# A perceiver layer with mixture-of-experts: four expert buffer sets, accumulating stores, new step orders

## The reference, cut to what matters

```python
x = x + xattn(layernorm(x), ctx)   # 16 heads, 64 batches of 32 queries on 257 context rows
x = x + attn(layernorm(x))         # causal, 16 query and 4 key heads of 16, ternary weights
x = x + moe(layernorm(x))
# moe: xt has T = 2048 rows of 256; 8 experts of capacity C = 256; hidden 352 (padded to 384)
probs = softmax(xt @ Wg); eidx = argmax(probs); gate = probs[eidx]
pos = rank of the row among the rows of its expert;  keep = pos < C
flat = where(keep, eidx * C + pos, E * C)
xd = zeros((E * C, d)).at[flat].set(xt, mode='drop')
oe = (silu(xd @ W1) * (xd @ W3)) @ W2                      # per expert
out = oe[min(flat, E * C - 1)] * (gate * keep) + silu(xt @ sw1) * (xt @ sw3) @ sw2
```

## Time and profile before

| | us |
|---|---|
| runs | 1545.86, 1538.57, 1541.29 |
| median | 1541.29 |
| profiled execution | 1538.1 |
| its span | 1536.3 |
| mean granted PE clock | 0.936 |

### The profile page before, as it was taken

How to read it: one execution, slowest core, us unless ns; L and a number is a source line. 1 busy time by engine, 2 the same in 40 slices (tenths; PEclk the granted TensorE clock), 3 DMA queues, 4 the chain that set the end, 5 groups by cost and what they waited for, 6 DMA issues and landing times.

```text
span 1536.3 us, 35628 instructions
## 1 busy us (share of the span) xinstructions
PE 1295.5 (84%) x10526; PEld 881.2 (57%) x10526; DVE 1005.7 (65%) x3748; ACT 841.6 (55%) x3560; POOL 538.5 (35%) x1337
## 2 busy tenths in 40 slices
PE   5768898989899898989898989888898989864881
PEld 2545666566666556565666565656565565643761
DVE  6846677677767677777777776777776767743112
ACT  5365566656475656666565666475656556631110
POOL 2044342524352534435243525342524325310003
PEclk9998999999999999999999999999999989985996
DMA  9000000000010101000001000000101000100544
GB/s 372 22 26 12 23 15 25 17 25 17 11 32 10 32 7 30 13 25 17 21 14 28 14 25 18 14 28 11 31 7 35 7 25 14 62 6 23 168 146 127
DMA packets 41191, 59.65 MB, mean 39 GB/s; under 512 B 5094, under 2 KB 35953, under 8 KB 40096
## 3 DMA queue, kind: packets, MB, share of 16 engines
q1 hardware_dynamic: 36880, 50.73, 10.3%
q0 software_dynamic: 2064, 6.14, 1.2%
q10 hardware_dynamic: 2176, 2.10, 0.4%
HBM read 48.62 MB, written 10.49 MB: 38 GB/s over the span
## 4 chain that ended last, share of the span: by engine, by line
PE 33%; issue 25%; POOL 16%; DVE 9%; ACT 5%; DMA 3%; POOLq 1%; SPq 0%; DVEq 0%; ACTq 0%
PE AB L594 21%; PE Eb L594 5%; POOL prob L1177 4%; PE Db L594 4%; ACT prob L1020 2%; DMA ctxn<-expert_rows 2%; POOL pjunk L1132 2%; PE C L719 1%; POOL cn_lo L1197 1%; DVE o_halves L1492 1%; POOL rstd L1152 1%; ACT rkb L1014 1%; POOL cl_rows L1212 1%; POOL c_lo L1138 1%; DVE kst L1312 1%
## 5 line engine op out<-in xcount | busy, mean ns | idle before, releaser
L950 ACT ACTIVATE AB<-AB 128x128 f32<-128x128 f32 (+1 forms) x1160 | 303.7, 262 | 185.4 <-PE AB L594 182.9
L1132 POOL TENSOR_TENSOR pjunk<-pjunk 128x1 f32<-128x1 f32 x288 | 56.3, 196 | 683.9 <-DVE sinv L1482 365.9
L594 PE MATMUL AB<-wk_hi,c_hi 128*128 128x512 f16 x512 | 199.7, 390 | 22.0 <-POOL c_lo L1138 8.8
L1312 DVE BATCH_NORM_STATS2 kst<-AB 128x6 f32<-128x256 f32 x512 | 181.3, 415 | 55.4 <-PE AB L594 50.9
L950 ACT ACTIVATION_READ_ACCUMULATOR AB<-AB 128x1 f32 (+1 forms) x1160 | 216.0, 186 | 0.0
L594 PE MATMUL AB<-wk_lo,c_hi 128*128 128x512 f16 x512 | 198.5, 388 | 0.0
L594 PE MATMUL AB<-wk_hi,c_lo 128*128 128x512 f16 x512 | 197.5, 386 | 0.0
L594 PE MATMUL AB<-ctxT,qpT 128*128 128x257 f32 x512 | 161.6, 472 | 35.5 <-DVE sc L1547 27.4
L1020 ACT ACTIVATE prob<-prob,nbias,rq 128x257 f32<-128x257 f32 x256 | 150.4, 590 | 7.9 <-DVE nbias L1477 7.9
L594 PEld LDWEIGHTS AB<-ctxT,qpT 128*128 128x128 f32 x512 | 115.2, 236 | 60.6 <-DVE sc L1547 29.1
L1177 POOL TENSOR_SCALAR prob<-prob,sinv 128x257 f32<-128x257 f32 x256 | 128.7, 503 | 20.2
(11 more groups left out here) (252 smaller groups left out, 2933.9 us busy)
## 6 DMA issues: line engine op xcount, KB each, us to landing
ctxT<-in_ctxT SPq DMA_DIRECT2D x64, 128.5 KB, 2.1
ctxn<-in_ctxn SPq DMA_DIRECT2D x64, 128.0 KB, 2.1
wq_hi<-in_w SPq DMA_DIRECT2D x4, 768.0 KB, 5.3
wq_lo<-in_w SPq DMA_DIRECT2D x4, 768.0 KB, 5.6
expert_rows<-base POOLq DMA_DIRECT2D x1, 2048.0 KB, 15.8
xin<-in_x SPq DMA_DIRECT2D x16, 128.0 KB, 2.2
prob<-in_wqT SPq DMA_DIRECT2D x1, 2048.0 KB, 19.2
xres<-in_x SPq DMA_DIRECT2D x16, 128.0 KB, 2.0
```

The source lines that it names most:

```text
L594: return pe.matmul(out, lhsT, rhs, start=start, stop=stop)
L950: ins = nc.scalar.activation(k, k, ACT.Square, accum_out=sums[0:m, h:h + 1])
L1132: own.mark(pool.tensor_tensor(pjunk[:, 0:1], pjunk[:, 1:2], pjunk[:, 1:2], ALU.mult))
L1312: ins = V.bn_stats(stats[:, 0, 2 * half + n], AB[0:m, 2 + half, 2 * D * n:2 * D * (n + 1)])
```

## The change

Three things.

Experts: four sets of buffers (`SETS`), made of weights and tiles that are free by then; loads of experts 2 and 3 are issued before the last tile ends. The expert loop is written out.

Output: with each row, the tile stores a second, 8-byte record (gate, token number) at the same slot of a DRAM table (`mark_rows`) by a second indirect DMA of 128 rows. The whole table is loaded once as `marks`. ACT multiplies each expert's rows by the gate as it drains them, and POOL adds them to `out` by an indirect DMA with `compute_op=ALU.add`, two of 128 rows for each expert. `expert_out`, gathers, read-back and final stores go.

Order: the tables of all four engines are new for the loop, and the last tile has a table of its own.

```diff
+SETS = 4
 ORDER = {
-    "PE": """K0 K1 pt3 K2 X K3 o3 Q f K4 rk0 xt1 K5 qkv QP K6 qk s0 rk1 sc s1 K7 pt0 pv s2 st pr rk2 o0 pt1 o1
-              xt2 s3 lg up pos rk3 dn pt2 o2""".split(),
+    "PE": """K0 pt3 K1 K2 X K3 o3 Q f rk0 K4 xt1 K5 qkv QP K6 qk s0 rk1 sc K7 s1 pt0 pv s2 pr rk2 st o0 pt1
+              xt2 s3 lg up pos o1 rk3 pt2 dn o2""".split(),
...
+    "ACT": """K0 ph3 K1 K2 X tl3 K3 oh3 Q K4 xt1 K5 qkv rk0 QP K6 qk e0 rk1 K7 sc e1 ph0 tl0 pv rk2 tl1 ph1 oh0
+              xt2 e2 up oh1 lg rk3 ph2 tl2 e3 oh2""".split(),
+    "DVE": """K0 X K1 dp3 K2 XL K3 do3 KN0 Q RQ f K4 K5 qkv K6 s0 sc K7 i0 s1 sm KN1 dp0 i1 ys s2 yv pr ln2 dp1 lg i2
+              do0 up pos do1 s3 dn dp2 i3 do2""".split(),
-    "POOL": """h1 h0 c2 n3 h2 X c3 r0 cl ln1 c0 h3 r1 n0 c1 r2 y n1 ln2 r3 n2 scat""".split(),
+    "POOL": """h2 h0 h3 h1 n3 X r0 ln1 cl r1 c0 c2 c1 n0 r2 y n1 ln2 c3 r3 n2 scat""".split(),
 }
+LAST_ORDER = {
+    "PE": "pt3 o3 f xt1 qkv qk sc pv st pr xt2 lg pos up dn".split(),
...
             store_base(LAST)
             sp.wait_ge(scattered.sem, scattered.at(LAST, "scat"))
+            load_rows(0)
+            load_rows(1)
+            sp.wait_ge(marked.sem, marked.at(LAST, "scat"))
+            sp.dma_start(marks[:]..., mark_rows...).then_inc(marks_in, 16)
...
                 pool.indirect_dma_start(xd_rows, ..., xn2[:], None, ...).then_inc(scattered.sem, 16)
+                pool.wait_ge(marked.sem, marked.before(p))
+                gate()
+                pool.indirect_dma_start(mark_rows, ..., slot_mark[:], None, ...).then_inc(marked.sem, 16)
...
+                for a in range(2):
+                    ins = nc.scalar.activation(eo[k][:, a], Db[:, DIM * a:DIM * (a + 1)], ACT.Copy, scale=marks[:, e, a, 0:1])
...
+            pool.wait_ge(base_out.sem, base_out.at(LAST, "o"))
+            for e in range(E):
+                pool.wait_ge(drained["D"].sem, drained["D"].at(p, f"dn{k}"))
+                for a in range(2):
+                    pool.indirect_dma_start(d["out"], ..., eo[k][:, a], None, ..., compute_op=ALU.add).then_inc(res_out[k][a], 16)
...
-                V.tensor_tensor(slots[:, bass.ds(p.tile, 1)], flat[:], keep[:], ALU.mult)
+                dve.wait_ge(marked.sem, marked.before(p))
+                own.mark(V.tensor_scalar(slot_mark[:, 1:2].bitcast(U32), token[:], 0.0, None, ALU.add))
```

More of the change, by code:

```diff
@@ L50 @@
 LK = 3 * (H // 4)
+SETS = 4
+NO_TOKEN = 1.0
 BELOW = -1.0e30
@@ L168 @@
 }
+LAST_ORDER = {
+    "PE": "pt3 o3 f xt1 qkv qk sc pv st pr xt2 lg pos up dn".split(),
+    "ACT": "ph3 tl3 oh3 xt1 qkv qk sc pv xt2 lg up".split(),
+    "DVE": "dp3 do3 f qkv sc sm ys yv pr ln2 lg pos up dn".split(),
+}
 def steps_of(engine, p):
@@ L174, in steps_of @@
         return START_ORDER[engine]
+    if p.kind == "last" and engine in LAST_ORDER:
+        return LAST_ORDER[engine]
     return [s for s in ORDER[engine] if p.kind == "full" or s in LATE]
@@ L563, in _ @@
             store_base(p)
+            sp.wait_ge(filled["5"].sem, filled["5"].at(p, "pt2"))
+            load_up(2)
+            load_down(2)
+            sp.wait_ge(filled["D"].sem, filled["D"].at(LAST, "f"))
+            load_up(3)
+            load_down(3)
             store_base(LAST)
             sp.wait_ge(scattered.sem, scattered.at(LAST, "scat"))
-            for k in range(2):
[L567 to L583, removed]
@@ L584, in _ @@
-            sp.wait_ge(res_out, 4 * 16)
+            load_rows(0)
+            load_rows(1)
+            sp.wait_ge(marked.sem, marked.at(LAST, "scat"))
+            sp.dma_start(marks[:].rearrange("p e a two -> p (e a) two"), mark_rows.rearrange("(n p) two -> p n two", p=P))\
+                .then_inc(marks_in, 16)
+            load_rows(2)
+            load_rows(3)
+            for e in range(SETS, E):
+                p, k = Period("expert", (e - SETS) // 2), e % 2
+                sp.wait_ge(filled["2"].sem, filled["2"].at(p, f"h{k}"))
+                load_up(e)
+                load_rows(e)
+                sp.wait_ge(filled["D"].sem, filled["D"].at(p, f"dn{k}"))
+                load_down(e)
@@ L915, in expert_down @@
                     for f in range(FC):
-                        ins = mm(Db[:, DIM * a:DIM * (a + 1)], ehT[k][:, f, P * a:P * (a + 1)], ew2[k][:, f],
+                        ins = mm(Db[:, DIM * a:DIM * (a + 1)], ehT[k][:, f, P * a:P * (a + 1)], ew2[e % SETS][:, f],
                                  start=f == 0, stop=f == FC - 1)
                 ins.then_inc(filled["D"].sem, 1)
[L920 to L935, removed]
+            expert_turn(0)
+            expert_up(0)
+            expert_turn(1)
+            for e in range(E - 1):
+                expert_up(e + 1)
+                if e + 2 < E:
+                    expert_turn(e + 2)
+                expert_down(e)
+            expert_down(E - 1)
         @block.scalar
@@ L1097, in expert_exp, with expert_out @@
                                      ACT.Tanh, scale=0.5).then_inc(sig_tanh.sem, 1)
[L1099 to L1115, removed]
-                expert_exp(q, 0)
-                expert_turn(q, 1)
-                expert_out(p, i, 1)
-            final = Period("expert", E // 2 - 1)
-            expert_exp(final, 1)
-            expert_out(final, final.i, 0)
-            expert_out(final, final.i, 1)
+            def expert_out(e):
+                p, k = Period("expert", e // 2), e % 2
+                act.wait_ge(marks_in, 16)
+                if e >= 2:
+                    for a in range(2):
+                        act.wait_ge(res_out[k][a], 16 * (e // 2))
+                act.wait_ge(filled["D"].sem, filled["D"].at(p, f"dn{k}"))
+                for a in range(2):
+                    ins = nc.scalar.activation(eo[k][:, a], Db[:, DIM * a:DIM * (a + 1)], ACT.Copy, scale=marks[:, e, a, 0:1])
+                ins.then_inc(drained["D"].sem, 1)
+            expert_turn(0)
+            expert_exp(0)
+            expert_turn(1)
+            for e in range(E - 1):
+                expert_exp(e + 1)
+                if e + 2 < E:
+                    expert_turn(e + 2)
+                expert_out(e)
+            expert_out(E - 1)
         @block.gpsimd
```

133 lines of the change are left out of this document (65 added, 68 removed).

## The result

| | before | changed |
|---|---|---|
| median of the runs | 1539.9 us | 1642.4 us (1641.4 to 1649.1, 4 runs) |
| profiled execution, span | 1538.1, 1536.3 us | 1642.5, 1640.5 us |
| ratio to before | | 1.067 (95% interval 1.063 to 1.071) |
| mean tile of the loop | 82.28 us | 91.67 us |
| first expert's row transposes to the end | 116.2 us | 80.2 us |

The changed kernel is slower. The loop lost 9.39 us per tile, about 141 us in 15; the part behind it won 36.0. The median before is of four runs here and of the first three in the table ahead of the prediction, so it is 1539.9 and not 1541.3.

A forecast was written before the change was run, and what follows sets the result against it. PE, 84% busy, was near the bound, waiting on other engines' in-order chains. 1538.1 + 123 (loop, 8.2 us per tile) + 15 (clock) - 37.0 (tail) = 1639.1, plus 3.2 for the median: 1642 us; own range 1575 to 1700, wider 1525 to 1700.

The forecast's parts named there:

- (a): Tile start: pt3 right after K0 waits for POOL's two splits and n3, PE stands still; 3.0 us lost per tile.
- (b): From sc to s2: the 1.89 us wait for s1 goes, later steps take nearly all; 0.4 us gained per tile.
- (c): From s2 to xn2: DVE does s2 ahead of yv, n1 precedes ln2 on POOL; 4.05 us lost per tile.
- (e): From slot_s to the next K0: the marks' second indirect DMA on POOL delays the splits; 1.3 us lost per tile.
- (f): PE's clock: the new gaps of 3.0 and 3.9 us can drop it to 1.2 GHz; 1 us per tile taken.
- tail: First expert's row transposes to the span's end: 116.2 us becomes 78.7 with four buffer sets and adding stores; gain 37.0.
- (d): From xn2 to slot_s: the gate's exponential is behind oh1 on ACT; 0.25 us lost per tile.
- Rival 1: Loop: new order as good as the old, marks included, slack takes up (a) and (c); 1504 us, chance 0.14.
- Rival 2: Loop: only the marks cost, 29 us against 37 gained; 1533 us, chance 0.07.
- Rival 4: Experts: adding stores take 8.1 us each, one after the other, 55 us more; 1697 us, chance 0.03.
- Rival 3: Loop: the clock falls in each tile behind both gaps, 6 us more; 1717 us, chance 0.11.

The follow-up runs named there:

- e2: The kernel before with only the four new loop lists, last tile's order kept: 1684.2 us, ratio to before 1.095.
- e5: The changed kernel with s2 on DVE behind ln2, and pt3 on PE and ph3 on ACT behind K1: 1552.1 us.
- e12: The changed kernel with needless products in four idle places of PE, ahead of pt0, pv, o0 and pt3, order untouched: 1596.5 us.
- e11: e1 with gate and token in the token's row (one indirect DMA), POOL's cleared-marks wait moved to the scatter, needless products ahead of s1, pv, s2: 1492.5 us.
- e6: The changed kernel with needless products on PE ahead of pt0 and pv only, order untouched: 1622.7 us.
- e13: e5 with needless products on PE ahead of pt0 and pv, five and six: 1522.5 us.
- e1: The changed kernel with the four loop lists of before; marks, buffer sets, accumulating stores and last tile's new order stay: 1522.3 us, ratio to before 0.990.
- e3: The changed kernel with only DVE's s2 moved from ahead of yv to behind ln2: 1589.9 us.

## Why the prediction was right, and where only the sum was

The forecast was 1642 us and the mechanism, two waits made by the order of the steps, is shown by e2 to e5. The terms were less exact than the total: in the loop it had 8.2 + 1 = 9.2 us, measured 9.39. That the total is right to the microsecond is luck: (a) was 1.2 us per tile too high, (b) 0.3 and the rest 1.1 too low, and these cancel. The prediction also gives two lower ends for its range, 1575 and 1525; the result lies within both.

| step | foreseen | measured |
|---|---|---|
| (a) K0 to sc | +3.0 | +1.76 |
| (b) sc to s2 | -0.4 | -0.08 |
| (c) to (e), s2 to K0 | +5.6 | +7.70 |
| (f) clock, in addition | +1 | in the row above |
| tail, first transpose to the end | 78.7 us | 80.2 us |

- (a) The gap ahead of `pt3` was foreseen at 3.0 and is 2.85, by the named releaser. That `Q` and `f` come as much later also held. But before, `xt1` waited 1.72 us for DVE's `xn`; now it waits 0.58. This slack took 1.1 us back, and the prediction had looked for none.
- (b) was a sum of small moves; it is nothing. The 1.89 us ahead of `s1` went, and waits ahead of `pt0` and `pv` (1.22 and 1.42 us) stand there instead.
- (c) The place was right (gap ahead of `o0` foreseen 3.9, found 4.34) and the size too small: from `s2`'s start on PE to `xn2`'s end 15.1 us, foreseen 12.1. The 12.1 were made of `s2` and `pr` at full clock. At half clock they are 1.79 and 0.87 us longer, 2.7 together where (f) had priced 3.6, and the new order has both on the way to `x`. (The 1.85 us taken for `s2` on DVE are those of `s3` in the earlier trace rows, which does the same for the fourth batch.)
- (d) `slot_s` comes 10.4 us behind `xn2`, foreseen 10.0.
- (e) 6.1 us from `slot_s` to `K0`, foreseen 6.5: the second DMA takes 1.39 us of POOL and not 1.91, since its wait behind the gate instruction is 0.16 and not 0.56 and the instruction itself 1.01 and not 1.12.
- (f) is the term that was mis-sized. By e12 the clock costs the changed kernel 3.2 us per tile, by e11 the old order 0.9 to 1.4, so the difference is about 2 and not 1. The reason lies in the choice of the tile: the earlier trace rows show `s2` at 2.00 us, but in 11 of the 14 tiles of before it took 2.9 to 3.7. The low clock at `s2` was there already and cheap, since little waited for `s2` (5.8 us to `o0` in the tile of the earlier trace rows, 6.5 in the mean). The change made that stretch hardly slower (mean 3.18 to 3.54 us), it put it on the path. Work put into the gaps ahead of `pt0` and `pv` takes this low clock away (e6, e13); the forecast's third rival stood on the gaps ahead of `pt3` and `o0`.
- Tail. Experts come every 8.21 us (foreseen 8.37 without waits), 72.0 us became 70.7 up to ACT's last drain. Behind it are 9.6 us instead of 6.7: each store's issue holds POOL for 1.55 us, taken as 1.12, and the span ends 6.1 us after the last one's start.

Rival 1 (the order neutral, 1504) is refuted by e2. Rival 2 (only the marks cost) is refuted by e1: with them the loop loses 1.1 us. Rival 4 (stores in series) is refuted by the trace: all eight drains of ACT wait for PE and none for a store, and experts come every 8.21 us. Rival 3 (the low clock behind both gaps, 6 us more) overstated it: of the 3.2 us 2.3 are at `s2` and `pr`, and by difference 0.9 are left for the two gaps. The 3 us that it had for the low clock over `pt3` and `K1` don't occur in the changed kernel; in the five tiles of e6 where `K1` has it, they are 1.6. The Trainium skill's page "TensorE: Matmul & The Clock Gate" ("What's actually happening") says that activity is what releases the throttle; the granted clock of 1.00 in e11 and e12, with nothing changed but more work on PE, agrees.

Open: the stage from `o0` to `K0` is 1.9 us longer in e2, e3, e12 and e13 than before, whether marks are there or not. Part of it are PE's short waits ahead of `xt2`, `pt2` and `o2` (0.76, 0.48 and 0.70 us in the changed kernel), but no run took them apart. In the one tile shown the stage is 2.67 us longer: 1.06 up to `xn2`'s end, 0.68 from there to `slot_s` and 0.93 on to `K0`. The 1.06 are mostly a matter of where the stage starts: `xn2` ends 5.06 us behind `yv`'s start (4.93 before), but `o0` starts 1.72 us behind it and not 2.65.

## What to carry to other kernels

In a hand-written order of in-order engines, follow every moved step to the last thing that it waits for, and ask what stands behind it: two moved steps, put back by three places and by one, gave back 52 and 40 us here. Read the stage in all of its turns before taking a duration from one, since an instruction that is slow but off the path in most turns becomes the bound when a move puts work behind it. Where a stretch at half the clock is on the path, needless work in PE's idle time bought 1.4 to 3.2 us a tile. But the low clock can move on to the next long gap: with two of four places filled it did (e6), and with the two long gaps gone two fills were enough (e13).

## What the hardware showed that was not expected

- An indirect store with add of 128 rows of 1 KB holds POOL for 1.55 us and 0.30 more to the next; the plain scatter of the same 128 rows takes 1.09, one of 128 rows of 8 bytes 1.01. So 128 times fewer bytes make the issue only 0.08 us shorter (no run varied the number of rows), and the add costs some 40% more. From issue to landing they take 3.9, 2.5 and 4.1 us (medians of 16 in the whole trace of the changed kernel; the single ones above are the last tile's). The small rows, issued right behind the others, take longest.
- A load of 16 KB in 8-byte pieces lands after 3.8 us (one load), longer than the 128.5 KB loads in rows of 1028 bytes (2.1, median of 64).
- In the tile shown the granted clock stayed at 1.00 through 4.3 us of idle time, was 0.84 over the next microsecond, in which PE worked again, and 0.50 over the one behind; in the same kernel it was 0.50 behind a stretch with many short gaps.
